# Four stages on one core: where three stage borders wait for stores, how the last expert tile reaches memory, and how the first tokens are loaded

## The reference

```
x = x + L0_attn(layernorm(x))      # 64x64 delta-rule memory, a scan over tokens
x = x + L0_ffn(layernorm(x))       # 8 experts 256-1024-256, the best 2 of each token, weighted
x = x + L1_attn(layernorm(x))      # RWKV: time mix (log-sum-exp recurrence), then channel mix
x = x + L1_ffn(x)                  # ternary weights: 256-1024-1024-1024-256, silu and gelu
# L1_attn, second half (channel mix):
xn = layernorm2(x); kk = xn @ W_cm; kk = kk*cmk + x_prev*(1-cmk)
rr = sigmoid(xn*cmr + x_prev*(1-cmr)); x = x + rr * (square(relu(kk)) @ W_cp)
```

## Time and profile before

| | us |
|---|---|
| median of 3 runs | 2169.77 (2169.62 to 2170.21) |
| the profiled execution, its own time | 2177.72 |
| its span, first to last instruction | 2175.9 |
| TensorE busy | 1965.3 (90%) |
| VectorE busy | 1354.6 (62%) |
| ScalarE busy | 975.4 (45%) |
| GpSimd busy | 247.8 (11%) |

### The profile page before, as it was taken

How to read it: one execution, slowest core, us unless ns; L and a number is a source line. 1 busy time by engine, 2 the same in 40 slices (tenths; PEclk the granted TensorE clock), 3 DMA queues, 4 the chain that set the end, 5 groups by cost and what they waited for, 6 DMA issues and landing times. The chain is left out here.

```text
span 2175.9 us, 32550 instructions
## 1 busy us (share of the span) xinstructions
PE 1965.3 (90%) x11554; PEld 1682.8 (77%) x11554; DVE 1354.6 (62%) x2760; ACT 975.4 (45%) x1777; POOL 247.8 (11%) x229
## 2 busy tenths in 40 slices
PE   7999999997399999996776749998999999999999
PEld 5799999996399999996544437776888888888887
DVE  7566677776466666665799877886345345344442
ACT  4655555553234444342788656662232233223221
POOL 0010012222333223232000000000000000000000
PEclk9999999996699999998888869999999999999999
DMA  3299311112444433223232331414000000000000
GB/s 102 85 357 408 113 48 57 57 58 98 154 88 101 87 78 79 49 42 70 69 88 60 94 98 58 174 68 155 1 20 1 19 19 0 20 19 0 20 10 11
DMA packets 86100, 170.36 MB, mean 78 GB/s; under 512 B 7216, under 2 KB 49840, under 8 KB 85808
## 3 DMA queue, kind: packets, MB, share of 16 engines
q1 hardware_dynamic: 65920, 132.47, 17.5%
q0 software_dynamic: 18176, 33.70, 7.7%
q10 hardware_dynamic: 1888, 2.67, 0.4%
HBM read 91.61 MB, written 88.74 MB: 83 GB/s over the span
## 5 line engine op out<-in xcount | busy, mean ns | idle before, releaser
L2642 ACT ACTIVATE x_tok<-bank,scl 128x512 f32<-128x512 f32 x128 | 88.3, 690 | 360.2 <-PE bank L2693 359.4
L2692 PE MATMUL bank<-hAh,ffn_h 128*128 128x512 f32 x512 | 202.7, 396 | 0.7 <-DVE x_tok L2570 0.7
L2692 PE MATMUL bank<-hBh,ffn_h 128*128 128x512 f32 x512 | 201.7, 394 | 0.0
L2693 PE MATMUL bank<-hAl,ffn_h 128*128 128x512 f32 x512 | 199.4, 389 | 0.0
L2693 PE MATMUL bank<-hBl,ffn_h 128*128 128x512 f32 x512 | 199.3, 389 | 0.0
L1475 POOL DMA_INDIRECT tokens_behind_spare_rows<-yg,row_of_token x72 | 133.1, 1848 | 318.5 <-DVE row_of_token L1635 298.3
L889 ACT ACTIVATE L<-bank 128x512 f32<-128x512 f32 x160 | 94.5, 595 | 139.4 <-PE bank L1151 129.6
L533 DVE TENSOR_TENSOR st<-st,bank 128x256 f32<-128x256 f32 x224 | 90.6, 419 | 99.7 <-PE bank L1158 87.6
L1151 PE MATMUL bank<-L 128*128 128x128 f32 x768 | 146.9, 281 | 0.0
L1158 PE MATMUL bank<-st,L 128*128 128x128 f32 x896 | 139.3, 282 | 4.7 <-DVE st L533 4.7
L1572 ACT ACTIVATE h<-bank,b1s 128x256 f32<-128x256 f32 x280 | 125.5, 471 | 36.3 <-PE bank L1403 29.3
(11 more groups left out here) (434 smaller groups left out, 5494.7 us busy)
## 6 DMA issues: line engine op xcount, KB each, us to landing
z_by_expert<-zero SPq DMA_DIRECT2D x64, 520.0 KB, 15.8
ckb<-in_ffn_dram POOLq DMA_DIRECT2D x32, 352.0 KB, 3.4
xg<-z_by_expert SPq DMA_DIRECT2D x36, 260.0 KB, 3.1
x_tok<-in_w_dram SPq DMA_DIRECT2D x8, 1024.0 KB
ffn_h<-ffn_copy SPq DMA_DIRECT2D x2, 4096.0 KB, 14.9
x_tok<-after_time_mix SPq DMA_DIRECT2D x15, 512.0 KB, 6.0
st<-in_w_dram SPq DMA_DIRECT2D x6, 1024.0 KB, 6.4
x_tok<-x_T SPq DMA_DIRECT2D x9, 512.0 KB, 4.2
```

The costliest lines, as they stand in the source:

```text
L2642: A_.activation(gq[:, m % 4, :], B[2 + m % 4][:, :], ACT.Gelu, scale=scl[:, off[nm] + m:off[nm] + m + 1]).then_inc(g_act, 1)
L2692: T.matmul(out, w, x[0], start=first, stop=False)
L2693: return T.matmul(out, w, x[1], start=False, stop=last)
```

## The change

1. **The last expert tile** has its own buffers, `yg_last` and `last_row_of_token`. Its row numbers are made before `y`, ScalarE no longer waits there for the scatter of the tile before, and each half is sent when its own scaling is done.
2. **First token block**: four DMAs of 128x256 in place of one of 128x4x256, each with its own semaphore; DVE takes the statistics of each chunk as it lands. Block 1 is loaded ahead of W_cm and W_cp. DVE makes the low part of W_tm before the first statistics. `tmp` is allocated earlier, so at another SBUF address.
3. **Time mix to channel mix**: SyncE's waits for all `xa_out` and `sx_out` leave the end of the time mix. In the channel mix each load of a block waits for the stores that it reads, and the weights h1 wait for all of them. TensorE makes two of the three products of the first four key tiles (`first_keys`) at the end of the time-mix block; `up` makes the third in the channel mix.
4. **Channel mix to last feed-forward**: SyncE waits before the barrier for `x3_out[0]` alone. The wait for `x3_out[1]` stands behind SyncE's first loads of the next block and behind DVE's first `gated`.
5. `deviation` names the table set that holds logarithm and exponential, so ScalarE loads one table where it loaded two: 70 table loads in the program in place of 78.

```diff
-            add_to_tokens(tile_count(pool))
+            total = tile_count(pool)
+            pool.wait_ge(to_rdy, total + 1)
+            for j in range(2):
+                pool.wait_ge(y_rdy, total * 2 + (j + 1))
+                pool.sem_inc(turn_seen, 1)
+                pool.indirect_dma_start(x2_d, bass.IndirectOffsetOnAxis(to_row_last[:, j:j + 1].bitcast(u32), 0), yg_last[:, j, :], None,
+                                        compute_op=ALU.add).then_inc(y_out, 16)
...
-            gated(total)
+            for j in range(2):
+                act.wait_ge(yb_rdy, total * 2 + (j + 1))
+                nc.scalar.activation(yg_last[:, j, :], yt[:, j, :], ACT.Copy, scale=own_g[:, 0, 0, j:j + 1]).then_inc(y_rdy, 1)
...
+            V.tensor_tensor(to_row_last[:, :], own_g[:, 0, 1, :], spare[:, :], ALU.max).then_inc(to_rdy, 1)
             y(NE - 1, total)
-            rows_of_tokens(total)
...
-            tokens(0)
+            for j in range(CPB):
+                sp.dma_start(x_tok[:, chunk(0, j), :], x2_blocks[0][:, j, :]).then_inc(first_ld[j], 16)
+            tokens(1)
...
-            sp.wait_ge(xa_out, 16 * NB)
-            sp.wait_ge(sx_out, 16 * NB)
...
-            variances(0)
             dve.wait_ge(wth_rdy, 1)
             V.tensor_tensor(wtm[1][:, :, :], wst, f32(wtm[0][:, :, :]), ALU.subtract).then_inc(wts_rdy, 1)
+            variances(0)
...
+            def first_keys():
+                pe.wait_ge(cw_rdy, 2)
+                pe.wait_ge(km_out, 3 * NB - 1)
+                pe.wait_ge(lnv, 1)
+                pe.wait_ge(xn_hi, 1)
+                for m in range(4):
+                    for k in range(KT):
+                        for n in range(2):
+                            T.matmul(B[2 + m][:, :], wcm[n][:, k, m * 128:(m + 1) * 128], XN0[0][:, k, :], start=k + n == 0, stop=False)
...
+                sp.wait_ge(xa_out, 16 * NB if lo == 0 else 16 * (lo // BT + 1))
                 sp.dma_start(IN[:, q, 0, :, :], xa[:, :, lo:lo + BT]).then_inc(cin_ld[q], 16)
...
+                sp.wait_ge(sx_out, 16 * (place(b) // BT + 1))
                 sp.dma_start(IN[:, q, 2, :, :], sx[:, :, place(b):place(b) + BT]).then_inc(csx_ld[q], 16)
...
+                if n == "h1":
+                    sp.wait_ge(xa_out, 16 * NB)
+                    sp.wait_ge(sx_out, 16 * NB)
...
-            for q in range(2):
-                sp.wait_ge(x3_out[q], 16 * (NB // 2))
+            sp.wait_ge(x3_out[0], 16 * (NB // 2))
...
             def deviation(b):
+                nc.scalar.preload_act_table_set(LOG_EXP)
                 act.wait_ge(var_ps, b + 1)
...
             gated(0, 0)
+            dve.wait_ge(x3_out[1], 16 * (NB // 2))
```

More of the change, by code:

```diff
@@ L1362, in build @@
         raw_g, own_g, sum_g = sb("raw_gates", [128, 2, ZW - D], to=pb), sb("own_gates", [128, 2, 2, 2], to=pb), sb("sum_gates", [128, 2], to=pb)
-        to_row = sb("row_of_token", [128, 2], i32, to=pb)
+        to_row, to_row_last = sb("row_of_token", [128, 2], i32, to=pb), sb("last_row_of_token", [128, 2], i32, to=pb)
         xT = [sb(f"xT{h}", [128, KT, TT], f32r, to=pb) for h in "hl"]
@@ L1367, in build @@
         yt = sb("yt", [128, 2, D], to=pb)
-        yg = sb("yg", [128, 2, D], to=pb)
+        yg, yg_last = sb("yg", [128, 2, D], to=pb), sb("yg_last", [128, 2, D], to=pb)
         xf = x_tok[:, :, :].rearrange("p c d -> p (c d)")
@@ L1695, in build @@
         x2_ld = [sem(f"token_block_loaded_{b}") for b in range(NB)]
+        first_ld = [sem(f"first_tokens_loaded_{j}") for j in range(CPB)]
         def chunk(b, j):
@@ L1710, in build @@
         mv3 = sb("mv3", [128, NC, 2], to=pc)
+        tmp = sb("wkv_tmp", [128, 7, KT, BT], to=pc)
         wtm = [sb(f"wtm{h}", [128, KT, 3 * D], f32r, to=pc) for h in "hl"]
@@ L1718, in build @@
         stt_ = sb("wkv_state", [128, 4, KT, BT + 1], to=pc)
-        tmp = sb("wkv_tmp", [128, 7, KT, BT], to=pc)
         dg = sb("diagonals", [128, 3 * KT, 128], to=pc)
@@ L1756, in tokens @@
                 sp.dma_start(x_tok[:, SLOT[b] * CPB:(SLOT[b] + 1) * CPB, :], x2_blocks[b]).then_inc(x2_ld[b], 16)
-            tokens(0)
+            for j in range(CPB):
+                sp.dma_start(x_tok[:, chunk(0, j), :], x2_blocks[0][:, j, :]).then_inc(first_ld[j], 16)
+            tokens(1)
             sp.dma_start(cst[0].rearrange("p (k n) -> p k n", k=KT), byk(A["W_cm"])).then_inc(cw_ld[0], 16)
             sp.dma_start(cst[1].rearrange("p (k n) -> p k n", k=KH), A["W_cp"].rearrange("(k p) n -> p k n", p=128)).then_inc(cw_ld[1], 16)
-            for b in range(1, 5):
+            for b in range(2, 5):
                 tokens(b)
@@ L1829, in variances @@
                 cs = slice(b * CPB, (b + 1) * CPB)
-                dve.wait_ge(x2_ld[b], 16)
+                if b >= 1:
+                    dve.wait_ge(x2_ld[b], 16)
                 for j in range(CPB):
+                    if b == 0:
+                        dve.wait_ge(first_ld[j], 16)
                     last = V.bn_stats(st3[:, b * CPB + j, :], x_tok[:, chunk(b, j), :])
@@ L2196, in _ @@
             first_variance()
+            first_keys()
         pblk.close()
@@ L2463, in up @@
                     pe.wait_ge(xn_rdy, b + 1)
+                if b == 0 and i < 2:
+                    for m in (2 * i, 2 * i + 1):
+                        for k in range(KT):
+                            last = nc.tensor.matmul(B[2 + m][:, :], wcm[0][:, k, m * 128:(m + 1) * 128], XN0[1][:, k, :],
+                                                    start=False, stop=k == KT - 1)
+                        last.then_inc(cm_ps, 1)
+                    return
                 for m in (2 * i, 2 * i + 1):
@@ L2525, in _ @@
                 sp.dma_start(f32(FW[n][:, :, :]), raw[n].rearrange("(k p) n -> p k n", p=128)).then_inc(fw_ld[n], 16)
+            sp.wait_ge(x3_out[1], 16 * (NB // 2))
             def store(b, lo):
```

## The result

The changed kernel takes 2151.69 us (median of 4 runs, 2149.72 to 2153.91), the kernel before 2169.99 (4 runs, 2169.62 to 2170.49) on the same chip: ratio 0.9916, 95% interval 0.9899 to 0.9933, or 18.3 us less. The forecast was 2158.5 (2154.8 to 2162.6). The direction was right; the gain is 7 us larger than forecast and lies outside the range. The profiled execution took 2149.7, its span is 2148.0.

What follows compares the result with a forecast made beforehand. One engine nearly always busy inside each late stage bounds the kernel, so gains come at borders: 2.1 + 3.0 + 0.5 + 4.0 - 0.1 + 1.8 = 11.3 us off the median 2169.8, giving 2158.5 us, range 2154.8 to 2162.6.

Steps and rivals of the forecast that it cites:

- The last tile, 2.1: Last expert tile to time mix: earlier row numbers, scaling and scatters bring the next stage 2.1 us forward.
- The first tokens, 3.0: Time mix start to first product: 3.0 us, from W_tm's low part 1.1, chunked statistics 1.0, earlier landing 0.9.
- The rival of loads that land later: Time mix start: last chunk lands 1.5 us later than the whole load did; gain 8.9, time 2160.9; chance 0.07.
- The clock at the first restart, 0.5: Time mix's first product: TensorE's half clock lasts 5.0 us in place of 6.0, worth 0.5 us.
- Time mix to channel mix, 4.0: This border: stage starts 4.7 us earlier, squares 5.5 earlier; TensorE starts the second block 4.0 us earlier.
- The half clock's 1.5: First channel-mix block: half clock behind TensorE's 7.4 us gap before the variance makes key 5 about 1.5 us later.
- Inside the channel mix, -0.1: Second channel-mix block's restart: TensorE's half clock, taken as the mean of 5.0 us, costs 0.1 us.
- Channel mix to feed-forward, 1.8: Border to the last stage: store wait of 2.4 us goes, clock term of -0.6; 1.8 us gained.
- The barrier did not wait for GpSimd's landing: Rival, time mix to channel mix: GpSimd holds the barrier until its DMA lands; gain about 7.5, time 2162.3; chance 0.06.
- the clock did not take the gain back: Rival, TensorE's restarts: each runs 6.9 us at half clock; gain 7.6, time 2162.2; chance 0.14.
- it did not stay down: Rival, channel mix: half clock through the first two blocks makes the kernel 16.7 us slower, 2186.5; chance 0.03.
- A change at a border cannot make those stretches shorter, but it moves them whole: Time mix, channel mix, last feed-forward: one engine is nearly always busy inside, so only three border terms count.

Runs made afterwards that it cites:

- e8: Changed kernel with the last expert tile handled as before, the new tiles left in place so that no address moves: 2155.81 us, ratio 0.9918.
- e6: Changed kernel with token block 0 in one load and block 1 loaded behind W_cm and W_cp: 2169.73 us, ratio 0.9915.
- e13: Changed kernel with one line moved, the load of block 1 behind W_cm and W_cp again; block 0 keeps its four loads: 2156.79 us, ratio 0.9930.
- e14: Changed kernel with block 0 in one load; block 1 stays ahead of W_cm and W_cp, W_tm's low part ahead of the statistics: 2155.31 us, ratio 0.9915.
- e5: Changed kernel without `first_keys`: all three products of the first four key tiles behind the barrier, moved waits kept: 2166.12 us, ratio 0.9898.
- e2: Changed kernel with its two new expert tiles allocated behind yg, so the others keep the addresses of the kernel before: 2161.49 us, ratio 0.9949.
- e12: Changed kernel with block 1 centred right behind receptance(0) and squared ahead of high(0, 0) in the first channel-mix block: 2148.85 us, ratio 0.9892.
- e3: Changed kernel with two unused 32-byte tiles that put TensorE's operands in channel mix and last stage at multiples of 64 bytes: 2151.55 us, ratio 0.9905.
- e9: Changed kernel with SyncE's wait for both x3 stores back ahead of the last stage and the moved waits dropped: 2163.05 us, ratio 0.9896.
- e1: Kernel before with only an unused 128x2 int32 tile added behind row_of_token, moving seven expert-stage tiles by 32 bytes: 2164.99 us, ratio 0.9967.
- e11: Changed kernel with one unused 32-byte tile ahead of the attention stage's tiles, which shifts them to multiples of 64 bytes: 2164.01 us, ratio 0.9898.

## Why the forecast had the sum and missed the time

- **The last tile, 2.1: right.** 2.08 in the traces, and `e8` gives it back. GpSimd's start 1.75 behind `yt` was forecast at 1.74.
- **The first tokens, 3.0: right, and by the steps forecast; what went unseen is a tie.** The last chunk was to land at S+4.1, the scales to start at S+6.3, DVE to be free at S+13 and the high part of `a3` to end at S+14.5. Measured are S+4.1, S+6.35, S+12.8 and S+14.6. The low part has its 1.1. `e6` was expected to show whether the landing counts, from the reading that all four chunks were there at S+3.2; that reading was wrong, since it took the merged row for one time. Two things were missed. In the trace before, DVE's list ended 0.2 behind `a3h` and was not read as a second chain, so the prediction did not say that block 1's place is what carries the gain: with block 1 behind the weights DVE's list ends no earlier than before (`e13`, `e6`). And the earlier landing was in part put down to W_cm, which no longer shares the engines. In `e13` W_cm stands right behind the four loads and the last chunk still landed at S+4.0; one load of the whole block landed at S+4.7 with W_cm behind it (`e6`) and with block 1 behind it (`e14`). So the order gives nothing to the landing; the four loads do.
- **The rival of loads that land later did not occur.** Nor did the rule for many small transfers in the Trainium skill (DMA: Bandwidth & Descriptors, section Rules for kernel authors), to coalesce them into one large transfer, decide here: the last of the four 128 KB loads landed 4.1 us after the first was issued, the one of 512 KB 4.7 to 5.2 after its issue. The Trainium skill's rule speaks of mostly overhead under 64 KB, and these loads are larger.
- **The clock at the first restart, 0.5: 0.3.** The half clock lasted 3.4 us in place of 6.0, less than the 5.0 taken, which at half price would be 1.3. The stage is only 0.3 shorter, and 220.2 to 221.7 in the other profiles. TensorE is not the busiest engine there (129.49 of 171.00 us, DVE 162.48), so half clock may cost less than its half; that was not tried alone.
- **Time mix to channel mix, 4.0: 3.8 measured.** The start (5.1 earlier against `XN0l`, forecast 4.7) and the gap of 7.4 with its half clock came as forecast. The 0.8 for the filled banks came as 0.35 in the block with 0.46 lost at the barrier (`e5`), since TensorE was not back at the full clock in time; where it was (`e2`, `e8`) the block has 0.7 to 0.8. The half clock's 1.5 was the visible part of a cost of 6.0 (`e12`): the wait itself was taken as given.
- **Inside the channel mix, -0.1: 0.8 gained.** The mechanism was right, the length was not: 5.0 us of half clock were taken at the second restart, in place of 4.8 before, and 2.9 came. Half of 1.9 is 1.0. The same rule holds through the other profiles. The stage takes 195.7 to 197.6 us there, its half clock lasts 2.9 to 6.2, and the stage less half of that is 194.2 to 194.6 in every one but `e3` (195.2).
- **Channel mix to feed-forward, 1.8: 1.4.** The forecast was 2.4 for the wait, less 0.6 for the clock behind the first product. The first product comes 1.77 earlier, which `e9` gives back, and the last stage is 0.4 longer. TensorE starts 1.5 behind the stage's start, not 0.9, and the half clock lasts 3.9 us, not 5.0, against 3.3 before.
- **The rivals.** The barrier did not wait for GpSimd's landing, the clock did not take the gain back, and it did not stay down. Two figures there are off by little: the second restart's price by its own 6.9 and 5.0 us is 0.95, not 0.85, and a gain of 14.5 from the median gives 2155.3, not 2155.0.
- **The step that failed: "A change at a border cannot make those stretches shorter, but it moves them whole".** The sentence names the three late stages, and the sum has a term for each border and none for the inside of the expert stage, without a reason given. A new tile was costed as the instructions that use it. Its 32 bytes also move the operands of the stage it lives in: 8.3 us in the traces, 7.0 by `e1`'s median. The prediction listed another length inside a stage as what would prove it wrong, and that is what came, ahead of the first border.
- **Trace against median.** The profiled execution of before lay 8 above its median. Its attention stage was 548.7 us; other profiles have 540 to 562, and on one chip 552 to 562, with the same code (in `e11` with the shifted tiles). Taking the sum from the median was right. What makes that stage scatter was not tried and stays open.

## What to carry to other kernels

When a change adds a tile, list which other tiles it moves and compare their addresses modulo 64 bytes before costing anything; an unused tile in the kernel before tests that alone. When a wait is shortened, walk each engine's whole list up to the handover: two chains that end within 0.2 us of each other need both edits, and one alone gives nothing. A row that merges several instructions gives the start of the first; before calling them all free of a wait, look at the last by itself. Before calling a difference of one or two us scatter, compare how long TensorE ran at half clock in the stage. A wait of 7 us in front of a restart costs more than its half clock, so ask first whether the awaited step can be put ahead of work that nobody waits for.

## What the runs showed of the hardware

- Products of 128x256 in fp32r take 119.7 ns with seven tiles of the expert stage 32 bytes off multiples of 64 bytes, and 116.7 to 116.9 at multiples, at the same granted clock. A shift by 32 bytes moves 128x512 products of the channel mix from 231 and 233 to 227 ns and leaves the last stage's (227) and attention's (112) alone. Why these and not those was not settled.
- Four loads of 128 KB, issued within 1.77 us, had all landed 4.1 us after the first issue (4.0 in `e13`); the one of 512 KB took 4.7 to 5.2.
- TensorE kept its full clock over a gap of 2.54 us (`e12`) and came back at 1.2 GHz behind every gap of 5.09 or more seen before and after the change. Behind the start of the second channel-mix block the half clock lasted 2.9 to 6.2 us in 15 profiles, and the stage grew by half of it.
